# Graph network on one Trainium2 core: layer 3 gathers float32r pairs of 2 KB and takes one 512-column product a slot

## The reference

```python
for W, b in ((W1, b1), (W2, b2), (W3, b3)):        # 256->512, 512->512, 512->256
    h = relu(segment_sum((h @ W)[src] * dinv[src] * dinv[dst], dst) + b)
out = layernorm(x + h)
```

## Time and profile before

| what | value |
|---|---|
| median of 3 runs | 2476.48 us |
| lowest, highest | 2473.55, 2477.83 us |
| span of the profiled execution | 2904.7 us |
| mean granted TensorE clock in it | 0.910 |

### The profile page before, as it was taken

How to read it: one execution, slowest core, us unless ns; L and a number is a source line. 1 busy time by engine, 2 the same in 40 slices (tenths; PEclk the granted TensorE clock), 3 DMA queues, 4 the chain that set the end, 5 groups by cost and what they waited for, 6 DMA issues and landing times.

```text
span 2904.7 us, 33204 instructions
## 1 busy us (share of the span) xinstructions
PE 2414.3 (83%) x10765; PEld 1582.4 (54%) x10765; DVE 846.7 (29%) x1155; ACT 721.3 (25%) x1501; POOL 1757.6 (61%) x1768
## 2 busy tenths in 40 slices
PE   7866687788888789789788888979888789899897
PEld 6744465556565566344343444434444367777676
DVE  8875122112121211222222222222221223333333
ACT  6411222222122221122121222212221023333332
POOL 4366655556555564666667666666666756555553
PEclk9778899999899999899899898989999889999999
DMA  5445555555555555667666676767767645556663
GB/s 184 140 127 185 162 146 159 150 153 160 150 152 155 160 156 153 189 205 207 203 200 208 190 211 203 215 193 204 210 202 224 199 137 157 150 147 184 183 195 97
DMA packets 219959, 508.70 MB, mean 175 GB/s; under 512 B 38444, under 2 KB 106915, under 8 KB 219827
## 3 DMA queue, kind: packets, MB, share of 16 engines
q0 software_dynamic: 117216, 365.08, 44.1%
q1 hardware_dynamic: 83955, 109.08, 11.1%
q10 hardware_dynamic: 18656, 32.75, 3.7%
HBM read 433.60 MB, written 73.16 MB: 174 GB/s over the span
## 4 chain that ended last, share of the span: by engine, by line
PE 52%; another core or an unknown queue 22%; issue 10%; DVE 6%; ACT 4%; POOL 3%; DMA 1%; ACTq 1%; POOLq 1%; DVEq 0%; SPq 0%
PE ps_acc L1668 11%; PE ps_d L1668 9%; PE ps_o L1717 6%; PE ps_acc L1664 5%; PE ps_d L1767 4%; PE ps_h L1756 4%; PE ps_T L1756 3%; POOL rows L739 3%; PE ps_e L1738 3%; PE ps_l L1738 3%; ACT rows_r L1447 2%; PE ps_d L1620 2%; PE ps_h L1708 2%; DVE sel L956 1%
## 5 line engine op out<-in xcount | busy, mean ns | idle before, releaser
L739 POOL DMA_INDIRECT rows<-table,idx x1249 | 1240.8, 993 | 709.2 <-issue 382.6
L739 POOL DMA_INDIRECT rows<-table_parts,idx x483 | 476.5, 987 | 336.1 <-PE ps_acc L1664 152.7
L1668 PE MATMUL ps_acc<-rows,sel 128*128 128x512 f32 (+2 forms) x1496 | 615.9, 532 | 61.8 <-DVE acc L1042 27.7
L956 DVE SCALAR_TENSOR_TENSOR sel<-ps_e,firsts,dstT 128x1152 f32<-128x1152 f32 (+1 forms) x214 | 302.5, 1414 | 1223.6 <-remote 430.6
L1668 PE MATMUL ps_d<-rows,sel 128*128 128x512 f32 (+2 forms) x1190 | 541.4, 571 | 13.0 <-DMA rows<-table,idx 9.2
L1668 PEld LDWEIGHTS ps_acc<-rows,sel 128*128 128x128 f32 x1496 | 300.8, 208 | 226.5 <-issue 172.4
L1668 PEld LDWEIGHTS ps_d<-rows,sel 128*128 128x128 f32 x1190 | 235.8, 206 | 171.1 <-issue 134.0
L1664 PE MATMUL ps_acc<-rows,sel 128*128 128x256 bf16 (+1 forms) x1533 | 252.3, 281 | 81.9 <-DVE acc L1042 66.8
L1717 PE MATMUL ps_o<-low,hT 128*128 128x512 f32 (+1 forms) x784 | 295.9, 523 | 27.2 <-ACT hT L1365 14.4
L1767 PE MATMUL ps_d<-big 128*128 128x256 bf16 x1470 | 241.1, 280 | 28.8 <-issue 28.6
L1756 PE MATMUL ps_T<-pairs_r,rows_r 128*128 128x512 f32 x686 | 236.2, 460 | 33.2 <-ACT rows_r L1447 21.6
(11 more groups left out here) (192 smaller groups left out, 1663.3 us busy)
## 6 DMA issues: line engine op xcount, KB each, us to landing
rows<-table,idx POOLq DMA_INDIRECT x1249
table<-made SPq DMA_DIRECT2D x49, 256.0 KB
acc<-table SPq DMA_DIRECT2D x49, 256.0 KB
built<-big SPq DMA_DIRECT2D x30, 384.0 KB
low<-built ACTq DMA_DIRECT2D x30, 384.0 KB
built_bytes<-big SPq DMA_DIRECT2D x54, 192.0 KB
low<-built_bytes ACTq DMA_DIRECT2D x54, 192.0 KB
table_parts<-big SPq DMA_DIRECT2D x24, 384.0 KB
```

Source lines behind the costliest of these rows:

```text
L739: pool.indirect_dma_start(out=to, out_offset=None, in_=its[0:nodes, :], in_offset=bass.IndirectOffsetOnAxis(ap=idx[:, of, k:k + 1], axis=0 ...
L956: v.scalar_tensor_tensor(to[:, k:k + FRONT, :], numbers.unsqueeze(1).broadcast_to([P, FRONT, P]), firsts[:, bass.ds(t, 1)], dstT[:, bass.d ...
L1668: return mm(to[:, 0:w], sel[:, k, :], rows_of[phase][:, k, 0:w] if first is None else first, start=start, stop=stop)
```

## The change

The table that layer 3 gathers from is written as pairs: 512 words to a row (256 high, 256 low), 2 KB in place of 1 KB. ACT writes the high part of a tile as float32r straight from PSUM at the end of layer 2; DVE makes the low part by one operation from the same PSUM tile (`take_low`) two windows later in its own order; SP stores both (256 KB a tile in place of 128 KB). The six turns of `take_apart` go. In layer 3 each slot makes one float32r product of 512 columns with float32r selection matrices, in place of one float32 product of 256; the window's sum is 512 wide, and `finish_pairs` adds high and low with one more DVE operation. Own rows are 256 KB in place of 128 KB. The ring of widened counts moves from `rows` (which now needs its whole width) to the place of the weights, and the loaded counts shrink from two whole tiles (8 pieces) to four piece buffers with a semaphore each: a piece is loaded one tile ahead in place of two. The byte counts that layer 2 builds move to another place.

```diff
+        table_pairs = nc.dram_tensor("table2_pairs", (T * P, 2 * C), F32).ap()
-        blocks = [loaded[:, b * T * P:(b + 1) * T * P].rearrange("p (h d) -> p h d", d=P) for b in range(2)]
+        loaded = [low[:, b * PIECE:(b + 1) * PIECE].bitcast(BF16) for b in range(len(PIECES))]
+        ring = [low_r[:, RING_AT + b * RING * P:RING_AT + (b + 1) * RING * P].rearrange("p (h d) -> p h d", d=P)
+                for b in range(2)]
...
# SP, own_rows
+                        if phase == 2 and per == 1:
+                            sp.dma_start(acc[:, :], table_pairs[bass.ds(t * P, P), :]).then_inc(own_in, 16)
# SP, store
                         if phase == 1 and per == 1:
+                            sp.wait_ge(low_ready, t + 1)
+                            sp.dma_start(table_pairs[bass.ds(t * P, P), :],
+                                         pairs[:, bass.ds(t, 1), :].rearrange("p a w -> p (a w)")).then_inc(stored, 16)
# POOL, gather
+                if in_pairs:
+                    to, its = rows_pairs[:, k, :].bitcast(F32), table_pairs
# DVE, take_sum
-                w = WIDTH[phase]
+                w = 2 * C if in_pairs else WIDTH[phase]
+            def finish_pairs(t, taken, used_to, seq):
+                v_.wait_ge(sum_taken, taken)
+                v.scalar_tensor_tensor(y1[:, :], acc[:, C:2 * C], dinv[:, bass.ds(t, 1)], b3b[:, :], ALU.mult, ALU.add).then_inc(y_scaled, 1)
+                v_.wait_ge(y_scaled, t + 1)
+                normalize(acc[:, 0:C], t, y1[:, :], acc_used, used_to, res[:, :], res_in, t, seq, y3[:, :], y3_free, y_ready)
-            def take_apart(turn, t, n):
...
+            def take_low(t):
+                v_.wait_ge(made_ready, nth(1, t) + 1)
+                v.scalar_tensor_tensor(pairs_r[:, bass.ds(t, 1), 1, :].rearrange("p a c -> p (a c)"), ps_o[:, 0:C],
+                                       dinv[:, bass.ds(t, 1)], pairs_r[:, bass.ds(t, 1), 0, :].rearrange("p a c -> p (a c)"),
+                                       ALU.mult, ALU.subtract).then_inc(low_ready, 1)
# DVE, layer 2: after steady of tile t (and so after its back half)
-                            take_apart(i - 1, n * (i - 1), n)
+                            take_low(ROUND * i + o - 1)
...
# DVE, to_next(1)
                     prepare_early(n, 0, to)
+                    if phase == 1:
+                        take_low(T - 2)
                     take_sum(phase, n - 1, n - 1, True, ps_sums[(n - 1) % 2] if phase > 0 else ps_acc)
                     indices(base, 1 - WINDOWS[phase + 1] % 2)
                     prepare_early(n, 1, to)
+                    if phase == 1:
+                        v_.wait_ge(late_ready, 1)
+                        take_low(T - 1)
# ACT, make and widen
-                    to = whole[:, bass.ds(t, 1), :].rearrange("p a c -> p (a c)")
+                    to = pairs_r[:, bass.ds(t, 1), 0, :].rearrange("p a c -> p (a c)")
-                act.wait_ge(blocks_in[d % 2], 16 * len(PIECES) * (DENSE_OF // 2 * g + d // 2 + 1))
+                act.wait_ge(blocks_in[piece], 16 * (j + 1))
-                    load_blocks(DENSE_OF * g + d + 2, d % 2, piece)
+                    load_block(j + 1, piece)
# PE, add_slot and product
+                if in_pairs:
+                    return mm(to[:, 0:2 * C], sel_r[:, k, :], rows_pairs[:, k, :] if first is None else first,
+                              start=start, stop=stop)
+                if lows is not None:
+                    pe.wait_ge(low_ready, lows)
```

More of the change, by code:

```diff
@@ L137, in gnn_program @@
         W3_AT = W2_AT + KH * HID
-        low = sb("low", [P, W3_AT + KH * C], I32)
+        LOW = W3_AT + KH * C
+        with nc.sbuf_tensor("low_r", [P, LOW], F32R) as low_r:
+            pass
+        low = sb("low", [P, LOW], I32)
         raw = low[:, 0:RAW].rearrange("p (i a b) -> p i a b", i=3, a=RA)
@@ L142, in gnn_program @@
         w3 = low[:, W3_AT:].bitcast(F32).rearrange("p (k n) -> p k n", n=C)
-        loaded = low[:, 0:T * P].bitcast(BF16)
-        blocks = [loaded[:, b * T * P:(b + 1) * T * P].rearrange("p (h d) -> p h d", d=P) for b in range(2)]
+        RING = PIECES[0][1]
+        PIECE = RING * P // 2
+        loaded = [low[:, b * PIECE:(b + 1) * PIECE].bitcast(BF16) for b in range(len(PIECES))]
+        RING_AT = len(PIECES) * PIECE
+        ring = [low_r[:, RING_AT + b * RING * P:RING_AT + (b + 1) * RING * P].rearrange("p (h d) -> p h d", d=P)
+                for b in range(2)]
+        assert RING_AT + 2 * RING * P <= LOW and all(hi_h - lo_h <= RING for lo_h, hi_h in PIECES)
+        HOTS = PER_HALF * (QUADS + P) // 2
+        BYTES = T * P // 4
+        making_bytes = [low[:, HOTS + b * BYTES:HOTS + (b + 1) * BYTES].bitcast(U8).rearrange("p (h d) -> p h d", d=P)
+                        for b in range(2)]
+        assert HOTS <= RAW and HOTS + 2 * BYTES <= W3_AT
         assert RAW * 2 <= T * P
@@ L178, in gnn_program @@
             "p (j c) -> p j c", j=HALVES)
[L182 removed]
+        with nc.sbuf_tensor("pairs_r", [P, T, 2, C], F32R) as pairs_r:
             pass
@@ L409, in gnn_program @@
         x_parts_stored = sem("x_parts_stored")
-        blocks_in = [sem(f"blocks_in{b}") for b in range(2)]
+        blocks_in = [sem(f"blocks_in{piece}") for piece in range(len(PIECES))]
         late_ready = sem("late_ready")
-        highs_ready = sem("highs_ready")
-        pairs_ready = sem("pairs_ready")
+        low_ready = sem("low_ready")
         widened = sem("widened")
@@ L1447, in widen @@
                 nc.scalar.activation(ring[piece % 2][:, 0:hi_h - lo_h, :].rearrange("p h d -> p (h d)"),
-                                     piece_in(DENSE_OF * g + d, d % 2, piece), ACT.Copy).then_inc(widened, 1)
-                if more:
+                                     piece_in(j, piece), ACT.Copy).then_inc(widened, 1)
+                if j + 1 < DENSE:
                     act.wait_ge(widened, whole_x + 1)
-                    load_blocks(DENSE_OF * g + d + 2, d % 2, piece)
+                    load_block(j + 1, piece)
             def deviation(t):
@@ L1548, in pieces @@
                         for x in xs:
-                            widen(g, x, not (last and x >= 2 * len(PIECES)))
+                            widen(g, x)
                     if not first:
@@ L1669, in add_slot, with slots @@
                           start=start, stop=stop)
-            def slots(phase, n, ks, first, need=None, beside=None, ps=None, in_parts=False):
+            def slots(phase, n, ks, first, need=None, beside=None, ps=None, in_parts=False, in_pairs=False):
                 to = ps_acc if ps is None else ps
@@ L1753, in dense @@
                         end = h == hi_h - 1
-                if first and d == 0 and h in [t0 for t0, _ in PAIRS_OF]:
-                    pe.wait_ge(pairs_ready, [t0 for t0, _ in PAIRS_OF].index(h) + 1)
-                ins = mm(ps_dense[into].rearrange("p (i c) -> p i c", i=2), counts_of, pairs_r[:, :, h, :], start=(h == 0), stop=(h == T - 1))
+                if first and d == 0 and (h == 0 or h >= T - 2):
+                    pe.wait_ge(low_ready, max(h + 1, T - 2))
+                ins = mm(ps_dense[into], counts_of, pairs_r[:, h, :, :].rearrange("p i c -> p (i c)"), start=(h == 0), stop=(h == T - 1))
                 if end:
```

140 lines of the change are left out of this document (61 added, 79 removed).

## The result

| | kernel before | kernel after |
|---|---|---|
| median of the runs, us | 2477.15 (2473.55 to 2483.09) | 2413.20 (2407.31 to 2417.67) |
| ratio, 95% interval | 1 | 0.9746 (0.9730 to 0.9762) |

The change takes off 64 us, 2.5%. The forecast was 2448 us, a gain of 29, within 2410 to 2490 us: the sign and the range held, but the gain that was forecast is less than half of the one that came. The profiled execution after spans 2405.6 us beside a timed 2407.31; the late signals that lengthened the profile of before to 2904.7 us are absent.

What follows compares the result with a forecast made beforehand. Layer 3 was taken to be bound by PE and its loop through DVE and ACT. Layer 3 -32, layer 2 +2 and the passage +1 gave -29 us, from 2476.5 to 2448 us, range 2410 to 2490.

Steps and rivals of the forecast that it cites:

- Engines loaded so evenly wait for each other, so I take 465: Layer 3 after: chains of PE 443, POOL 430 to 451, DMA 406 to 466 us give 465, from 497 before.
- the turns of `take_apart`, also some 20 us, go; DVE is busy for 296 of 1198 us, so 0: Layer 2: DVE's added low-part operations, 24 us, and its removed turns, some 20 us, change the time by 0.
- PE loses 79 us: Layer 3: PE's products fall from 477 to 398 us, a slot costing 0.23 us in place of 0.45.
- Undisturbed stage before: Layer 3 of the kernel before, without late signals: 477 + 20 for edges and waits for ACT = 497 us.
- The loop over ACT: Layer 3 tile ends: DVE's longer work and PE's shorter piece cost up to 1.4 us a place, 25 us in all.
- POOL: Layer 3: 337 gathers at 1.25 to 1.31 us, 421 to 442; chain 430 to 451 us, no longer hidden behind PE.
- DMA: Layer 3: the doubled gathered bytes make DMA a third bound at 406 to 466 us.
- Passage and counts: Between layers 2 and 3: net +1 us, bounds -2 to +4; layer 3's later loads of counts stay covered.
- three signs of being wrong: Layer 3 gathers faster than 1.2 us, ACT's widening waiting for counts in many places, layer 2 growing over 10 us.
- PE's whole gain arrives: Rival: gathers' 0.30 us gap is the recorder's, PE's chain alone decides layer 3, 2400 to 2425 us; chance 0.17.
- no change: Rival: 2476 us, as DMA fills layer 3, ACT's loop sets the pace, or the new product is no cheaper; 0.13.
- slower: Rival: DMA bounds layer 3 and can't be filled; 2500 us at a share of 0.81; chance 0.18.

Runs made afterwards that it cites:

- e2: Changed kernel with layer 3 storing, loading and gathering only 1 KB of each pair, low halves of gathered tiles left out: 2410.82 us.
- e4: Changed kernel with 84 of 337 gathers of layer 3 left out, their products taking the rows of the slot before: 2413.92 us.
- e1: The kernel before, unchanged, profiled once more: span 2471.7 us, ratio 0.9990.
- e5: Changed kernel with five of VectorE's turns put back into layer 2, on data they leave unchanged: 2423.14 us, ratio 0.9785.
- e9: Changed kernel with VectorE kept as busy at the places of five turns in layer 2, by operations with one operand in PSUM: 2410.80 us.
- e6: Changed kernel with ACT's order in layer 3 altered, pieces 1, 2, 7, 12 and 15 of a group widened ahead of the deviation: 2401.21 us, ratio 0.9699.
- e7: Changed kernel with pieces widened ahead of the deviations in layer 3 and 84 gathers left out there: 2375.54 us.
- e8: Changed kernel with VectorE's old, shorter work at gathered tiles' ends (low halves left out) and slots 4, 7, 10, 13 not gathered: 2393.39 us.

## Why the prediction was wrong in size

**The step that failed first: "Engines loaded so evenly wait for each other, so I take 465".** Of the three chains, PE's at 443 us set the time: 442.0 were measured. The 22 us on top, up to near the tops of POOL's 451 and DMA's 466, were an analogy with layer 2, and nothing of them came: taking a quarter of the DMA engines' load away (e2) or a quarter of POOL's work (e4) moved the stage by 0.7 us. In this stage, chains beside each other with buffers between them cost their longest, not more. Layer 2, the row that the step leaned on, is 8% longer than PE's busy time in e1 and not 18% (1037.1 to 958.8 us), so more than half of what the analogy rests on came with the first profile and its late signals. The 8% have another reason: gathers fill the layer. After the change 785 of them at 1.25 us are 981 us, and the stretched ones add 35 (the time above 0.95 us), 1016 of its 1023.

**The step that failed second: "the turns of `take_apart`, also some 20 us, go; DVE is busy for 296 of 1198 us, so 0".** It priced VectorE's work by VectorE's idle time and not by what it does to POOL, which layer 2 hangs on. Measured: 13.8 us less where the sum had 2 more; e5 and e9 show the cause. The prediction took it that PE waits for gathered rows there seldom. That was so in the first profile, with its late signals: 21.1 us in 14 places. In e1 it is 75.7 us in 51:

```profile
PE ps_acc L1668 <- DMA rows<-table,idx: 39.5, 24, 4.7
PE ps_d L1668 <- DMA rows<-table,idx: 36.2, 27, 3.5
```

Between the gain of 29 that was forecast and the 66 of the spans, 23 us are the first step (465 for 442.0), 16 the second, 2 the passage, and the stage before, 4.5 us shorter than put, takes 4.5 back.

- **PE, right.** 0.23 us for a slot: in the timeline under e6, a slot at 2067.12 and the next dense product at 2067.35. "PE busy in layer 3 near 415" was 404. "PE loses 79 us" shows in e7: without the loop and with POOL out of the way the stage is 86 us under before, some 7 of them waits that stood there already.
- **Undisturbed stage before, right:** 497 put, 492.5 measured (e1). That the late signals were the profile's alone was an inference; e1's span of 2471.7 us bears it out.
- **The loop over ACT, right in place, near in size.** Of PE's 79 us some 28 were lost here and not to "what POOL and DMA no longer hide". The sum had 25 us for what the loop grows by, beside 20 for edges and the waits that stood there before. Those 20 measure 15.5 in e1 (492.5 less 477). With the whole loop at some 35 (e7) and edges at 8, 43 less 15.5, the growth is about 28. That VectorE's longer ends make most of it shows in e8, with 19 us; the shrinking of PE's piece, the other half of the term, was not tried by itself.
- **POOL, right as a chain, wrong as a term.** 430 to 451 us; e6 shows it at 434.8. In the change as made it is covered by PE's chain. The upper price, 1.31 us a gather, was a misreading: layer 2's mean of 1008 ns comes from the gathers stretched beside VectorE (in e1 45.5 of the 793.7 us of all gathers), not from rows of 2 KB, which layer 3 now gathers in 0.95 us each.
- **DMA, too dear.** 406 to 466 us were put; 0.90 of 442 are 398. The queue of the gathers carried 86.93 MB at 57.9% of the stage, 2.94 us a MB, where the prediction had taken 3.46 from layer 2 (3.38 in e1; why layer 2 pays more is open):

```profile
q0 software_dynamic: 26530, 86.93, 57.9%
```

  The stage moved 307 GB/s. The Trainium skill, "DMA: Bandwidth & Descriptors", section Specifications, with its 358 GB/s, was the better guide here: by it DMA binds nothing, and nothing here was bound by DMA. As a limit the trace doesn't bear the figure out: single fortieths of this stage moved up to 397 GB/s.
- **Passage and counts.** The passage gained 1.4 us where 1 was to be lost. The counts' four buffers cost nothing: in e6, which takes pieces earlier, no wait for a widened piece stands among PE's waits. None of the three signs of being wrong came: gathers go out every 1.251 us, ACT's widening waits for no counts, and layer 2 shrank; the signs didn't cover what happened.
- **The rivals.** "PE's whole gain arrives" named 2400 to 2425 us, and the time fell in it. Its stage, PE's chain alone up to 443 us, is what came, but its reason, that the 0.30 us between gathers is the recorder's doing, did not hold: e6 stops at POOL's 1.251 us a gather, and fewer gathers (e7) then take 26 us off the timed runs too. Without layer 2's 13.8 us, which it didn't have, the time would have been 2427, so its hit is in part luck. Of "no change", the part by which the loop over ACT sets the pace came true for 28 of PE's 79 us. The parts by DMA, and "slower", needed DMA at its limit; a share of 0.90 was reached without harm.

## What to carry to other kernels

When several chains run side by side with buffers between them, as in this one stage, take the longest as the stage's time and add nothing for their being close; what is close decides only how soon the next gain stops (7 of 35 us in e6). After making an engine faster, look at what the engine that feeds it waits for in its own order: moving work that was ready ahead of a wait took 7 us more off the stage (12 between the medians). Price removed work by whom it holds up, not by its own engine's idle time. And before taking a ratio from a profile that is 17% longer than the timed runs, profile the kernel once more.

## What the runs showed of the hardware

A VectorE operation that casts from SBUF to SBUF, or takes two operands in SBUF, holds up a gather that POOL begins during it: 0.95 us became 2.31 and 3.09 beside a cast of 1.75 and a subtraction of 3.36 us, and both gathers ended 0.82 to 0.83 us after the operation. Operations of VectorE with an operand in PSUM did not (e9). The Trainium skill, "SBUF — State Buffer", section "SBUF: two separate sides", says it: the two engines have one pair of ports in common, held for a whole instruction, and POOL can't write a DMA's descriptors while VectorE has it. The trace agrees. The kernel after still has such operations in layer 2, the comparisons that make the one-hots for the counts (128x3136 and 128x2048). The 35 us of stretched gathers named above all lie in 36 gathers that begin during one of 128x3136, such as this one:

```profile
1304.16 1.78 DVE L1144 TENSOR_TENSOR low<-away,lo 128x3136 bf16<-128x3136 bf16 x1
1304.32 2.44 POOL L758 DMA_INDIRECT rows<-table,idx  x1 [0.30 <-issue]
```

That they cost layer 2 as much was not tried.
